# Weighted graph pass: GpSimd's mid-group wait for four gathers replaced by a wait for the scatter at the group's end

## The reference

```python
messages = edge_val[:, None] * embeddings[edge_src]
neighbor_emb = jax.ops.segment_sum(messages, edge_dst, num_segments=embeddings.shape[0])
interaction_emb = neighbor_emb * embeddings
side_emb = (neighbor_emb + interaction_emb) @ W2.T + b2
```

```python
e = jax.nn.leaky_relu(a_src[src] + a_dst[dst], negative_slope=0.2)
...
agg = jax.ops.segment_sum(msg, dst, num_segments=M).reshape(M, HEADS * NUM_EXPERTS) + b_gat
```

## Time and profile before

| | us |
|---|---|
| median of 3 runs | 8996.98 (8985.14 to 9004.04) |
| the profiled execution, its own time | 9013.4 |
| its span, first to last instruction | 9011.7 |
| GpSimd busy | 5432.2 (60% of the span) |
| TensorE matmul busy | 5737.0 (64%) |
| VectorE busy | 3945.5 (44%) |
| ScalarE busy | 1582.5 (18%) |

### The profile page before, as it was taken

The page is one execution under the profiler, slowest core; times in us unless marked ns, Lnnn a source line. Parts: engine busy times, 40 slices in busy tenths (PEclk is TensorE's granted clock), DMA queues, the critical chain, the costliest instruction groups (busy, mean ns, idle before and its releaser), DMA issues. The chain is left out here.

```text
span 9011.7 us, 116542 instructions
## 1 busy us (share of the span) xinstructions
PE 5737.0 (64%) x27644; PEld 4852.9 (54%) x27645; DVE 3945.5 (44%) x10109; ACT 1582.5 (18%) x3574; POOL 5432.2 (60%) x5690
## 2 busy tenths in 40 slices
PE   3677777777773488880555444444446588888894
PEld 2555565555553377770343333333335587878783
DVE  4566666777777300005444433343435322222225
ACT  1122222122120233330000000000001233333331
POOL 3666666666665566656666666666666555555562
PEclk7787777787875699995777777676768578788886
DMA  3333333333333244443333222222220222222235
GB/s 111 90 89 88 88 90 87 88 89 88 89 86 101 74 146 143 144 136 112 89 89 89 86 80 79 80 80 80 79 80 21 57 59 63 59 62 61 60 64 164
DMA packets 426058, 793.32 MB, mean 88 GB/s; under 512 B 129162, under 2 KB 267134, under 8 KB 425684
## 3 DMA queue, kind: packets, MB, share of 16 engines
q0 software_dynamic: 235504, 474.87, 20.5%
q1 hardware_dynamic: 190436, 317.20, 10.4%
HBM read 720.67 MB, written 70.98 MB: 88 GB/s over the span
## 5 line engine op out<-in xcount | busy, mean ns | idle before, releaser
L1153 PE MATMUL g_pM<-g_G,g_S 128*128 x3328 | 1215.7, 544 | 1533.6 <-ACTq L1047 999.0
L833 POOL DMA_INDIRECT g_G<-table,X x1664 | 1578.0, 948 | 931.3 <-issue 458.4
L843 POOL DMA_INDIRECT g_G<-table,g_IDX x1616 | 1534.7, 950 | 879.9 <-issue 525.1
L1153 PEld LDWEIGHTS g_pM<-g_G,g_S 128*128 128x128 f32 x3328 | 931.0, 287 | 1818.3 <-issue 1616.1
L1121 PE MATMUL g_pM<-g_G,g_S 128*128 128x260 f32 x3328 | 1261.7, 539 | 697.2 <-DVE acc L950 679.7
L1697 POOL DMA_INDIRECT q_G<-table,slot x1072 | 1035.1, 966 | 724.6 <-issue 272.2
L1121 PEld LDWEIGHTS g_pM<-g_G,g_S 128*128 128x128 f32 x3328 | 826.1, 266 | 989.2 <-DVE acc L950 765.9
L958 DVE TENSOR_TENSOR acc<-g_pM,acc 128x256 f32 x1664 | 695.6, 418 | 1357.7 <-PE g_pM L1153 587.6
L618 POOL DMA_INDIRECT slots<-sort_PAIR,sort_ADDR x1024 | 1014.4, 991 | 455.1 <-issue 294.5
L950 DVE TENSOR_TENSOR acc<-g_pM,acc 128x260 f32 x1664 | 711.7, 428 | 275.3 <-PE g_pM L1121 89.3
L938 DVE TENSOR_SCALAR g_S<-iota,g_REL,g_WT 128x128 f32<-128x128 f32 x1664 | 587.8, 354 | 187.3 <-issue 172.5
(11 more groups left out here) (335 smaller groups left out, 6877.4 us busy)
## 6 DMA issues: line engine op xcount, KB each, us to landing
e_W<-in_L_ffn_W SPq DMA_DIRECT2D x210, 512.0 KB
sort_PAIR<-slot_rows SPq DMA_DIRECT2D x66, 512.0 KB
g_G<-table,X POOLq DMA_INDIRECT x1664
g_G<-table,g_IDX POOLq DMA_INDIRECT x1616
ys_all<-ew_Y SPq DMA_DIRECT2D x196, 128.0 KB
sm_Y<-ys_all SPq DMA_DIRECT2D x28, 896.0 KB, 10.7
q_ST<-slot_rows SPq DMA_DIRECT2D x34, 512.0 KB
sort_ADDR<-slot_rows SPq DMA_DIRECT2D x34, 512.0 KB
```

The source lines that it names most:

```text
L833: pool.indirect_dma_start(G[:, r, u, :], None, table, bass.IndirectOffsetOnAxis(ap=IDX[:, k * GRP + u:k * GRP + u + 1].bitcast(U32), axis= ...
L843: pool.indirect_dma_start(G[:, r, u, :], None, table, bass.IndirectOffsetOnAxis(ap=IDX[:, g * GRP + u:g * GRP + u + 1].bitcast(U32), axis= ...
L1153: m = pe.matmul(pM[r % 2 * 2 + half][:, u % HG, :], S[:, r, u, :], rows.rearrange("p a d -> p (a d)"), start=True, stop=True)
```

## The change

Three things change in the text, one of them in behaviour. `place` takes the number of scatters between two waits in place of a flag; the two functions that waited after every fourth scatter pass 4, and do what they did. In the weighted pass, a group that has a scatter no longer waits after its fourth gather. It waits after its scatter, until that scatter has landed. Groups 0 to 71, which have no scatter, keep their wait in mid-group.

```diff
             if sort is not None:
-                sort.place(pool, count, pausing=True)
+                sort.place(pool, count, pause_every=4)
...
-    def place(self, pool, count=NTF, pausing=False):
+    def place(self, pool, count=NTF, pause_every=0):
...
-            if pausing and t % 4 == 3:
+            if pause_every and t % pause_every == pause_every - 1:
                 pool.wait_ge(self.s_placed[j], (t // (2 * GRP) * GRP + t % GRP + 1) * 16)
...
-                    if u == HG - 1:
+                    if u == HG - 1 and g < TG - place:
                         pool.wait_ge(gather_done[r], (g // RINGS + rounds0) * 16 * GRP + 16 * HG)
                 if g >= TG - place:
-                    sort.place(pool, 1)
+                    sort.place(pool, 1, pause_every=1)
```

## The result

The changed kernel takes 9059.73 us (median of 6 runs, 9019.93 to 9082.57). The kernel before, run in turn with it on the same chip, takes 8986.51 us (8984.10 to 9004.04). The ratio is 1.0075, with a 95% interval of 1.0051 to 1.0098. The change makes the kernel 73 us slower, where 84 us less was forecast. The profiled execution has a span of 9052.6 us (9011.7 before), 41 us more: the pass is 59 us longer in it, and the last layer's gathers (line 1697, the same code) happened to take 20 us less, 7192.0 to 8921.7 against 7132.2 to 8881.4.

A forecast was written before the change was run, and what follows sets the result against it. GpSimd's own issue work and mid-group wait were taken to bound the weighted pass. 230 us saved, less 143 for scatter waits and 3 for room, gave 84 us off 8997: 8913 us, range 8900 to 8975.

The forecast's parts named there:

- The mid-group waits, -230 us: GpSimd in the weighted pass: removing 130 waits after the fourth gather saves 1.77 us each, 230 us.
- The scatter's wait, +143 us: GpSimd behind each scatter: a 1.41 us wait, 1.11 us beyond normal spacing, 129 times, adds 143 us.
- Rival B: Scatter's wait behind gathers takes as long as a gather's, 2.05 us; 226 us come back, 8996 us, no change; chance 0.08.
- Longer bursts at nothing: GpSimd's queue: 13 transfers between drains only at the seam, otherwise still 9, so longer bursts cost nothing.
- "The margin holds in the ordinary groups", +3 us: Consumers TensorE and VectorE keep up with 12.40 us groups; GpSimd's late starts for room grow only from 9.0 to 12 us.
- Rival C: TensorE's sums held until GpSimd's queue drains, so every group waits 3.0 us for room: +307 us, 9304 us; chance 0.07.
- lower end, 8901: Larger gain if GpSimd's late starts for room vanish: 9 us more, 8901 us; chance 0.03.

The follow-up runs named there:

- no_wait: Changed kernel without the wait after the scatter, so neither wait in the 130 scatter groups: 8999.27 us, 1.0015 of the kernel before; repeated in another job, 8392.73 us, 0.9736.
- end_wait_third: Changed kernel, but waiting at the group's end for its eight gathers, ahead of the scatter, instead of for the scatter: 8883.28 us, 0.9995 of the kernel before.
- no_wait_at_all: Changed kernel with no pause in any group of the weighted pass, groups 0 to 71 included: 8896.72 us, 1.0001 of the kernel before; in another job 8282.26 us, 0.9590.
- scatter_in_middle: Changed kernel with the scatter and its wait moved behind the group's fourth gather: 8541.22 us, 0.9905 of the kernel before; repeated in another job, 9029.3 us, 1.0052.

## Why the prediction was wrong

- **The mid-group waits, -230 us: right in size.** They are gone from 130 groups. On chips without held queues no_wait gains 230 us.
- **The scatter's wait, +143 us: right.** It is 1.41 us in 57 groups of the profile after, and 1.41 us in all 129 where queues aren't held. Rival B is out: these writes to DRAM come back after 1.41 us, with eight gathers before them too. The Trainium skill, DMA: Bandwidth & Descriptors, "Anatomy of one DMA — SWDGE (gpsimd) path", calls the receipt of a write heaviest when the target is HBM, the DRAM of this kernel. The trace doesn't bear that out for these transfers: the wait is 1.41 us for the writes to DRAM and 2.07 us for the gathers into SBUF, though a gather has DRAM to read as well, so the receipt alone isn't measured. The about 2.0 us of fixed cost that the same section of the Trainium skill gives for a DMA from GpSimd isn't refuted: counted from the start of its issue, the scatter takes 0.99 + 1.41 = 2.40 us.
- **Longer bursts at nothing: right** for GpSimd's own gathers, 0.30 us apart behind four as behind eight, 4 us over the sum in 910 of them.
- **"The margin holds in the ordinary groups", +3 us: this step failed.** It should have been +3 + 143 us. I judged the consumers by their busy time, 6.0 and 5.1 us a group, and worked out that rows come 1.8 us earlier for 1.3 us less of cycle. But rows weren't what TensorE's results waited for. The earlier trace rows had it in plain sight: a step whose matmuls last 5.4 us gave its first sums 8.6 us after its start. I took it for a lag at a boundary of node blocks. But where queues aren't held the first sums of no step take over 3.9 us, boundary or not, so it was a late word. The trace before has 10 such steps over 7 us among 134, and the trace after has 34.
- **Rival C was the one that came true, milder.** It said that it decides once over 28 of 130 groups wait for room behind the scatter, at 3.0 us each beyond the scatter's wait. It was 61 groups, at (237.7 / 61) - 1.41 = 2.5 us each: 61 x 2.5 = 152 us, against the gain of 84. It had a chance of 0.07, though the earlier trace rows showed its mechanism at work.
- **The size of the range.** It reached to 8975 and left C out whole. (Its lower end, 8901, is 12 us under the forecast and not the 9 us that the text names: it takes back the 3 us of growth as well.) The result is 85 us above its end. A mechanism that one row of the trace shows at work deserved more than a few per cent, and a milder form of it inside the range.

What is shown: the loss exists in each job where the kernel before takes 8895 to 8992 us (1.0075, 1.0074, 1.0072), and in the one with 8651 us the change gains nearly what the sum said (77 of 84 us). In the first, instructions of idle queues last up to 1.4 us and TensorE's words come late; in the second neither. It is not shown that the held queues are why the words are late: the holds are in the queues of ScalarE, VectorE and SyncE, and the late word is TensorE's, whose own queue shows no hold. Both are absent in ten traces. In the other ten all have holds, and nine have first sums over 7 us after the step's start. That speaks for a common cause, no more, and the tenth, end_wait_third, speaks against a simple link: its VectorE and SyncE queues are held, and no first sums take over 5.1 us.

In that condition a group of 9 transfers took 13.0 to 13.1 us even with none of GpSimd's own waits (no_wait, no_wait_at_all), and the kernels with a pause of 2.05 us in the middle or 2.08 us at the end, which need 13.04 us by themselves, took the same. So the removal of the pause could gain nothing there. Whether 13.1 us is a limit, or two sums that happen to meet, these runs don't tell. The pause of 1.41 us left is worse than either none or 2.05 us, by 0.5 us a group. The waits show where the 0.5 us is: room costs the change 237.7 us and no_wait 243.0, so the same, and the change waits 1.1 us too long for its scatters in 57 of the other groups on top, and in the 11 unnamed starts. Where both meet, the sums came 2.4 us into a pause, so a pause that ends at 1.41 us is followed by another 1.7 us for room. Why the waits for room are the same without any pause stays open (in no_wait, 36 of VectorE's 89 long waits ended 3 to 4 us after GpSimd had stopped for room).

Also open: what keeps the words back and holds the queues, and whether that is a trait of a chip, of its condition at the time or of other work on it. Half the bytes left 0.46% of loss, and more room gave 1.09%. There is no trace of the kernel before from a chip without holds, so the comparison there is one of times alone.

**The best version** is no_wait_at_all: 0.9590 (0.9574 to 0.9606) where queues aren't held, 1.0001 (0.9986 to 1.0017) where they are. Its gathers, where the gain is:

```profile
L843 POOL DMA_INDIRECT g_G<-table,g_IDX x1616: 945/949/1035, 3972.6 to 6174.3; - x180
...
  issue: 492.3, 1615
```

All 1615 gathers behind the first come at the plain spacing of 0.30 us, and the whole pass is GpSimd's issue work.

## What to carry to other kernels

Don't judge a consumer's margin by its busy time. Take the time from the start of its step to the moment the next engine can use the result, in an ordinary group and in the worst one; where that is far above the busy time, something else has the slack in hand, and a shorter cycle of the producer turns into waits for room. When a wait is shortened rather than removed, ask who uses the pause, and run the version with no wait at all beside it. And where a small edit loses against a sound sum, run both kernels again in another job, on another chip if there is one, and compare the time of the kernel before first: here four kernels were at first read against a machine in another condition.

## What was not expected of the hardware

The same program takes 8623 to 8651 us in some jobs and 8895 to 8992 us in others, 3 to 4% more, at the same mean clock in the pass (0.71 and 0.70), and one change has opposite signs in them: 0.9911 and 1.0075. Whether the chips differ or their condition does is open, as chip number 3 stands for both. The difference isn't in the pass alone. Two rows of the dense expert stage, whose code is the same in both kernels, from no_wait (before takes 8992 us) and from scatter_in_middle (8625 us):

```profile
L2380 PE MATMUL e_pH<-e_XT,e_W 128*128 128x128 f32 x3360 | 410.8, 282 | 174.7 <-ACT e_XT L2324 166.8 <-issue 7.7
```

```profile
L2380 PE MATMUL e_pH<-e_XT,e_W 128*128 128x128 f32 x3360 | 394.5, 276 | 2.5 <-ACT e_XT L2324 2.5
```

The matmuls last 282 and 276 ns, but TensorE is idle 174.7 us before them in the one, 166.8 of it for ScalarE's tiles, and 2.5 us in the other. The longest durations of a queue's trivial instructions tell the two apart in each of the 20 traces here: ScalarE's assertions take at most 29 ns in the ten from the faster jobs, and up to 712 to 1417 ns in the other ten.
